# A row-maximum phase: its eight rounds rolled into loops, and the turn of the maxima moved from VectorE to TensorE

## The reference

```
xn   = layernorm(x)                                  # 4 x 2048 x 256
q, k, v = split(xn @ Wqkv.T); 16 heads of 16
dots = q k^T / 4, causal; attn = softmax(dots)
a    = (attn v) @ Wout.T + bout
h    = silu(fp4(xn) @ fp4(w_gate).T) * (fp4(xn) @ fp4(w_up).T)   # 704 wide
out  = x + a + fp4(h) @ fp4(w_down).T
```

## Time and profile before

| | |
|---|---|
| median of 3 runs | 2762.52 us (2760.96 to 2763.7) |
| the profiled execution's own time | 2762.52 us |
| its span | 2760.8 us |
| granted TensorE clock, mean over the span | 0.978 of full speed |
| busy: PE, DVE, ACT, POOL | 2562.2, 1934.7, 2038.4, 722.6 us |
| shift phase: first difference product to last join on DVE | 252.7 to 963.2 us |
| main phase: first score product | 996.4 us |

### The profile page before, as it was taken

One profiled execution on the slowest core, in us unless ns is written; L12 is line 12 of the kernel. 1 busy time (PEld: TensorE's weight loads), 2 busy tenths in 40 slices (PEclk: granted clock), 3 DMA queues, 4 the chain that ended last, 5 costly groups with the idle time before them and its releaser, 6 DMA issues.

```text
span 2760.8 us, 58289 instructions
## 1 busy us (share of the span) xinstructions
PE 2562.2 (93%) x18228; PEld 1304.5 (47%) x18228; DVE 1934.7 (70%) x5533; ACT 2038.4 (74%) x3502; POOL 722.6 (26%) x550
## 2 busy tenths in 40 slices
PE   2995999999999859999999999999999999999999
PEld 1883444444444424444454444444444445444455
DVE  7995999999999935655645656655656654566555
ACT  1554999999999847777758777775777775777775
POOL 3563334433333221122111112111121111212111
PEclk7997999999999979999999999999999999999999
DMA  2785555555445342202222112123022031220200
GB/s 70 238 272 123 75 75 75 76 72 71 71 70 72 45 84 38 51 19 39 47 78 48 32 31 46 29 58 80 22 42 43 21 76 50 40 47 23 41 24 32
DMA packets 118622, 175.70 MB, mean 64 GB/s; under 512 B 25648, under 2 KB 95024, under 8 KB 117808
## 3 DMA queue, kind: packets, MB, share of 16 engines
q1 hardware_dynamic: 97392, 147.33, 28.6%
q10 hardware_dynamic: 16576, 15.73, 2.1%
q0 software_dynamic: 4352, 8.92, 1.3%
HBM read 129.37 MB, written 42.53 MB: 62 GB/s over the span
## 4 chain that ended last, share of the span: by engine, by line
PE 54%; ACT 4%; issue 4%; SPq 1%; DMA 1%; DVE 0%; ACTq 0%; POOL 0%; DVEq 0%; POOLq 0%
PE O L923 17%; PE S L907 15%; PE F L943 10%; PE F L983 5%; ACT probs L1052 4%; PE F L973 2%; PE S L994 2%; PE S L910 2%; SPq L528 1%; PE F L936 1%; DMA y<-in_L_attn_x_dram 1%; DMA q_st<-s_shift 0%; DVE o_turned L1258 0%; ACTq L1047 0%; ACT xt_hi L1077 0%
## 5 line engine op out<-in xcount | busy, mean ns | idle before, releaser
L1052 ACT ACTIVATE probs<-S 128x1024 f32<-128x1024 f32 (+3 forms) x1280 | 1074.5, 897 | 227.6 <-PE S L910 84.1
L907 PE MATMUL S<-q_st,k_st 128*128 128x512 bf16 (+3 forms) x2560 | 648.8, 351 | 75.0 <-DMA q_st<-s_shift 38.4
L730 ACT ACTIVATE m_excess<-m_DIFF 128x512 f32<-128x512 f32 (+7 forms) x1536 | 647.1, 472 | 88.3 <-PE m_DIFF L690 42.3
L748 DVE CUSTOM_DVE_ANT_0 m_excess<-m_S,m_excess 128x512 f32<-128x512 f32 (+7 forms) x1536 | 700.7, 530 | 11.7 <-PE m_S L690 9.2
L923 PE MATMUL O<-probs,v_sb 128*32 128x512 f32 (+3 forms) x5120 | 603.6, 543 | 2.2 <-POOL v_sb L1129 2.2
L688 PE MATMUL m_S<-m_k,m_q 128*128 128x512 bf16 (+7 forms) x1536 | 483.1, 325 | 26.7 <-DVE m_row_max L748 17.3
L688 PE MATMUL m_DIFF<-m_k,m_q_diff 128*128 128x512 bf16 (+7 forms) x1536 | 478.0, 319 | 29.5 <-DMA m_q_diff<-s_q 29.2
L907 PEld LDWEIGHTS S<-q_st,k_st 128*128 128x128 bf16 x2560 | 213.7, 98 | 418.2 <-ACT probs L1052 235.1
L632 POOL TENSOR_TENSOR m_q_diff<-m_zero,m_q 48x4096 bf16<-48x4096 bf16 x32 | 224.4, 7011 | 429.0 <-DMA m_q<-s_q 418.3
L688 PEld LDWEIGHTS m_S<-m_k,m_q 128*128 128x128 bf16 x1536 | 148.3, 97 | 275.8 <-DVE m_row_max L748 194.9
L1246 DVE TENSOR_TENSOR ht_lo<-F,ht_hi 128x512 fp32r<-128x512 f32 (+1 forms) x128 | 71.0, 557 | 232.5 <-ACT ht_hi L1067 232.5
(11 more groups left out here) (163 smaller groups left out, 4189.8 us busy)
## 6 DMA issues: line engine op xcount, KB each, us to landing
k_st<-s_k SPq DMA_DIRECT2D x96, 256.0 KB, 8.6
q_st<-s_q SPq DMA_DIRECT2D x384, 64.0 KB
s_q<-a_part SPq DMA_DIRECT2D x48, 256.0 KB, 3.0
s_k<-a_part SPq DMA_DIRECT2D x48, 256.0 KB, 2.2
m_q<-s_q SPq DMA_DIRECT2D x96, 128.0 KB, 3.8
m_k<-s_k SPq DMA_DIRECT2D x96, 128.0 KB, 6.7
m_q_diff<-s_q SPq DMA_DIRECT2D x96, 128.0 KB, 8.1
m_k<-s_k SPq DMA_DIRECT2D x96, 124.0 KB, 5.2
```

The source lines that it names most:

```text
L730: act.activation(excess[u % MAX_EXCESS][:, 0:keys // 2], DIFF[u % MAX_BUFS][:, 0:keys // 2], ACT.Relu) \
L748: dve.tensor_tensor_reduce(larger, S[u % MAX_BUFS][:, 0:keys // 2], larger, 1.0, -3e38, ALU.add, ALU.max, column).then_inc(reduced[u % MAX ...
L907: ins = pe.matmul(S[half][:, s % 2, 0:st.width], k_st[p][:, s, st.j * P:(st.j + 1) * P], q_st[st.c % 2][:, s, st.skip:QC], start=True, sto ...
L1052: act.activation(probs[half][st.n % 2][:, :, 0:st.width], S[half][:, :, 0:st.width], ACT.Exp, scale=SCALE).then_inc(exped[half], 1)
```

## The change

1. The Python loops over batches and rounds of the shift phase become loops on the engines (`Fori`), on PE, ACT, DVE and SP as a loop over B with a loop over rounds in it, on POOL as one loop over the first seven rounds with the eighth behind it. Waits on semaphores inside compare with register values.
2. PE turns the table of maxima with one matmul against the identity at the end of each round, into the last difference bank (`turn`, which is `DIFF[3]`). It waits for DVE's join before it.
3. ACT makes the first part from that bank (a copy with scale -1 to bf16), and DVE the second part (`-turn - part0`). POOL's three operations and the tile `row_turned` go.
4. POOL writes each part with one transfer of 128 x 128 elements, two instead of eight per round. The wait of DVE for POOL's negation is replaced by a wait of ACT for `stored`.
5. PE waits for the last round's second part (`part1`) before the first use of `DIFF[3]` in a round.

```diff
--- before.py
+++ after.py
@@ -582,18 +582,17 @@
                               two("m_k", [P, MAX_LOAD, T], BF16))
         excess = [sb(f"m_excess{u}", [P, MAX_KEYS // 2]) for u in range(MAX_EXCESS)]
         row_max, second_max = sb("m_row_max", [P, MAX_HEADS, NKB]), sb("m_second_max", [P, MAX_HEADS, NKB - split])
-        row_turned, minus_max = sb("m_row_turned", [P, P]), sb("m_minus_max", [P, P])
-        shift_part = [sb(f"m_part{k}", [P, P], BF16) for k in range(SHIFT_PARTS)]
+        shift_part = [sb(f"m_part{k}", [MAX_HEADS * NKB, P], BF16) for k in range(SHIFT_PARTS)]
         ident_bf, future, zero = sb("m_ident", [P, P], BF16), sb("m_future", [P, P], BF16), sb("m_zero", [P, 1], BF16)
         S = [ctx.enter_context(nc.psum_tensor(f"m_S{u}", [P, MAX_KEYS // 2], F32)) for u in range(MAX_BUFS)]
         DIFF = [ctx.enter_context(nc.psum_tensor(f"m_DIFF{u}", [P, MAX_KEYS // 2], F32)) for u in range(MAX_BUFS)]
+        turn = DIFF[MAX_BUFS - 1][0:MAX_HEADS * NKB, 0:P]
         consts, zeroed, stack_ld, stack_free = once("m_consts"), [once(f"m_zeroed{p}") for p in range(2)], sems("m_stack_ld"), sems("m_stack_free")
         q_ld, q_negated = sems("m_q_ld"), sems("m_q_negated")
         differed, exceeded = sems("m_differed", MAX_BUFS), sems("m_exceeded", MAX_BUFS)
         scored, reduced = sems("m_scored", MAX_BUFS), sems("m_reduced", MAX_EXCESS)
-        joined, turned, negated, part0, part1, shift_st = (
-            sem("m_joined"), sem("m_turned"), sem("m_negated"), sem("m_part0"), sem("m_part1"), once("m_st"))
-        shift_dmas = SHIFT_PARTS * (P // SLOT)
+        joined, turned, part0, part1, stored, shift_st = (
+            sem("m_joined"), sem("m_turned"), sem("m_part0"), sem("m_part1"), sem("m_stored"), once("m_st"))
         aside = once("m_aside")
         rounds = H // MAX_HEADS
         loads = MAX_HEADS // MAX_LOAD
@@ -632,42 +631,31 @@
                 pool.tensor_tensor(q_diff[p][rows, :, :], zero[rows, 0:1].unsqueeze(2).to_broadcast([MAX_ROWS, MAX_LOAD, T]),
                                    q_st[p][rows, :, :], ALU.subtract).then_inc(q_negated[p], 1)
 
-            def store(n, negates):
-                for p in range(2):
-                    pool.wait_ge(q_negated[p], negates + PRIMED)
-                pool.wait_ge(turned, n + 1 + PRIMED)
-                pool.tensor_tensor(minus_max[:, :], zero[:, 0:1].to_broadcast([P, P]), row_turned[:, :], ALU.subtract) \
-                    .then_inc(negated, 1)
-                pool.wait_ge(negated, n + 1 + PRIMED)
-                pool.sem_inc(aside, 1)
-                pool.tensor_copy(shift_part[0][:, :], minus_max[:, :]).then_inc(part0, 1)
-                pool.wait_ge(part0, n + 1 + PRIMED)
-                pool.tensor_tensor(shift_part[1][:, :], minus_max[:, :], shift_part[0][:, :], ALU.subtract).then_inc(part1, 1)
+            def store(n):
                 pool.wait_ge(part1, n + 1 + PRIMED)
                 for k in range(SHIFT_PARTS):
-                    rows = dram["shift"][k, bass.ds(n * MAX_HEADS, MAX_HEADS), :].rearrange("h (i t) -> (h i) t", t=P)
-                    for a in range(P // SLOT):
-                        at = slice(a * SLOT, (a + 1) * SLOT)
-                        pool.dma_start(rows[:, at].rearrange("(c r) s -> r c s", r=SLOT),
-                                       shift_part[k][at, :].rearrange("r (c s) -> r c s", s=SLOT)).then_inc(shift_st, 16)
-                pool.wait_ge(shift_st, n * (16 * shift_dmas) + 16 * shift_dmas)
+                    pool.dma_start(dram["shift"][k, bass.ds(n * MAX_HEADS, MAX_HEADS), :]
+                                   .rearrange("h (i t) -> (h i) t", t=P), shift_part[k][:, :]).then_inc(shift_st, 16)
+                pool.wait_ge(shift_st, n * (16 * SHIFT_PARTS) + 16 * SHIFT_PARTS)
+                pool.sem_inc(stored, 1)
 
             pool.wait_ge(consts, 5)
             for load in range(2):
                 negate(0, load)
-            for n in range(B * rounds - 1):
+            with pool.Fori(0, B * rounds - 1) as n:
                 for load in range(2, loads):
                     negate(n, load)
                 for load in range(2):
                     negate(n + 1, load)
-                store(n, loads_before(n + 1, 1) + 1)
+                store(n)
             for load in range(2, loads):
                 negate(B * rounds - 1, load)
-            store(B * rounds - 1, loads_before(B * rounds, 0))
+            store(B * rounds - 1)
+
         @block.sync
         def _(sp):
-            for b in range(B):
-                for r in range(rounds):
+            with sp.Fori(0, B) as b:
+                with sp.Fori(0, rounds) as r:
                     n = b * rounds + r
                     for load in range(loads):
                         p = load % 2
@@ -697,6 +685,8 @@
                     pe.wait_ge(stack_ld[load % 2], loads_before(n, load) * (16 * load_dmas) + 16 * load_dmas + PRIMED)
                     pe.wait_ge(q_negated[load % 2], loads_before(n, load) + 1 + PRIMED)
                 pe.wait_ge(exceeded[u % MAX_BUFS], uses(n, u - MAX_BUFS, MAX_BUFS) + PRIMED)
+                if u == MAX_BUFS - 1:
+                    pe.wait_ge(part1, n + PRIMED)
                 product(DIFF[u % MAX_BUFS], q_diff[h // MAX_LOAD % 2], h, i, k0, keys // 2,
                         future[:, PAIR:P] if k0 + keys == (i + 1) * P else None).then_inc(differed[u % MAX_BUFS], 1)
 
@@ -708,8 +698,8 @@
                         future[:, 0:PAIR] if k0 + keys == (i + 1) * P else None).then_inc(scored[u % MAX_BUFS], 1)
 
             pe.wait_ge(consts, 5)
-            for b in range(B):
-                for r in range(rounds):
+            with pe.Fori(0, B) as b:
+                with pe.Fori(0, rounds) as r:
                     n = b * rounds + r
                     for u in range(MAX_LEAD):
                         differences(n, u)
@@ -718,10 +708,13 @@
                             differences(n, u + MAX_LEAD)
                         scores(n, u)
 
+                    pe.wait_ge(joined, n + 1 + PRIMED)
+                    pe.transpose(turn, row_max[:, :, :].rearrange("p h i -> p (h i)"), ident[:, :]).then_inc(turned, 1)
+
         @block.scalar
         def _(act):
-            for b in range(B):
-                for r in range(rounds):
+            with act.Fori(0, B) as b:
+                with act.Fori(0, rounds) as r:
                     n = b * rounds + r
                     for u, (h, i, k0, keys, _) in enumerate(round_units):
                         act.wait_ge(differed[u % MAX_BUFS], uses(n, u, MAX_BUFS) + PRIMED)
@@ -729,14 +722,17 @@
                         act.wait_ge(reduced[u % MAX_EXCESS], uses(n, u - MAX_EXCESS, MAX_EXCESS) + PRIMED)
                         act.activation(excess[u % MAX_EXCESS][:, 0:keys // 2], DIFF[u % MAX_BUFS][:, 0:keys // 2], ACT.Relu) \
                             .then_inc(exceeded[u % MAX_BUFS], 1)
+                    act.wait_ge(turned, n + 1 + PRIMED)
+                    act.wait_ge(stored, n + PRIMED)
+                    act.activation(shift_part[0][:, :], turn, ACT.Copy, scale=-1.0).then_inc(part0, 1)
 
         @block.vector
         def _(dve):
             for p in range(2):
                 for stack in (q_diff[p], q_st[p], k_st[p]):
                     dve.memset(stack[:, :, :].bitcast(F32), 0.0).then_inc(zeroed[p], 1)
-            for b in range(B):
-                for r in range(rounds):
+            with dve.Fori(0, B) as b:
+                with dve.Fori(0, rounds) as r:
                     n = b * rounds + r
                     for u, (h, i, k0, keys, second) in enumerate(round_units):
                         larger = excess[u % MAX_EXCESS][:, 0:keys // 2]
@@ -751,10 +747,9 @@
                         dve.wait_ge(reduced[buf], uses(n, len(round_units) - 1, MAX_EXCESS) + PRIMED)
                     dve.tensor_tensor(row_max[:, :, split:NKB], row_max[:, :, split:NKB], second_max[:, :, :],
                                       ALU.max).then_inc(joined, 1)
-                    dve.wait_ge(joined, n + 1 + PRIMED)
-                    dve.wait_ge(negated, n + PRIMED)
-                    dve.transpose(row_turned[:, :], row_max[:, :, :].rearrange("p h i -> p (h i)")).then_inc(turned, 1)
-                    dve.wait_ge(turned, n + 1 + PRIMED)
+                    dve.wait_ge(part0, n + 1 + PRIMED)
+                    dve.scalar_tensor_tensor(out=shift_part[1][:, :], in0=turn, scalar=-1.0, in1=shift_part[0][:, :],
+                                             op0=ALU.mult, op1=ALU.subtract).then_inc(part1, 1)
 
 
 class Step:
```

## The result

| | before | after |
|---|---|---|
| median, us | 2762.8 (2760.96 to 2763.7) | 2816.2 (2815.15 to 2817.19) |
| ratio | | 1.0188, interval 1.0175 to 1.0201 |
| span of the profiled execution, us | 2760.8 | 2810.2 |
| joins of rounds, first to last, us | 343.6 to 962.9 | 347.1 to 1020.5 |

The change costs 53.4 us. The forecast was +31.7, and 2816.2 lies above its range. The direction and the place were right. One term of the sum was too small.

What follows compares the result with a forecast made beforehand. DVE was taken to bound the shift phase. Per passage 3.9 + 0.7 + 0.5 + 0.2 = 5.3 us, for seven 37.1, less 5.45 at the phase's end, gives +31.7 on 2762.52: 2794.2 us, range 2772 to 2814.

Steps and rivals of the forecast that it cites:

- The bound and the place: Shift phase: DVE sets the pace from the first product on, and its idle time adds to the phase one to one.
- The handover: End of each round, join to turn to both parts: without branch cost, DVE starts again 1.07 us later than before.
- The fetch by itself: Loop branches at each round's end: DVE and ACT stall as in the main phase, DVE starting 3.9 us later than before.
- two things are added to each passage: From each round to the next: code fetch meeting other traffic, 0.7 us, and restarting without a lead, 0.5 us.
- the fetch meets other traffic: Branch at each round's end: code fetch runs beside SP's loads, 0.7 us a passage, bounded by 0 and doubling the 3.1 us.
- The restart of 0.5 us: Start of each next round: lost lead and PE's possibly lower clock cost 0.5 us a passage, between 0 and 1.4.
- the 0.2 for it: PE's loop branch at each round's end: 0.2 us a passage for the chance that this branch is dear.
- The end: End of the shift phase: earlier parts, six fewer transfer issues and a shorter drain save 5.45 us, between 3.95 and 7.9.
- the signs: Trace after: 93.8 us between joins, seven DVE idle times of 3 us or more, clock dips, end some 5 us shorter.
- The rival that DVE alone stalls: Branches at rounds' ends: only DVE waits for code, ACT and PE are ready; +26.5 us, 2789 us, chance 0.15.
- The heavy rival: Rounds' ends: fetch collides with loads and the clock falls, 8.4 us a passage, +53, 2816 us; chance 0.13.

Runs made afterwards that it cites:

- with the loads held: Changed kernel, with SP holding the second load of a round until DVE has reduced unit 3 of that round: 2796.2 us, 1.0123 to the kernel before.

## Why the prediction was wrong

- The bound and the place were right: DVE sets the pace, and each passage costs it what it stands idle.
- The handover was right: part 1 was over at J + 1.45 (forecast J + 1.1 to 1.4), and without loops DVE was back at J + 1.66 to 2.46 (forecast J + 1.85).
- The fetch by itself was right: J + 4.54 to 4.70 with the loads held, where I had 4.7. The stalls of the main phase's bodies of 1007 and 1030 instructions carried over to 634 and 437 (2.8 to 2.9 and 2.5 us with the loads held).
- **The step that failed** is the first of "two things are added to each passage": the fetch meets other traffic. I had 0.7 us, between 0 and 3.1. It is 7.80 - 4.62 = 3.2 us, just past its upper end. Seven times 2.5 us too little is 17 of the 22 us that are missing. I had the row for it: the DMA engines at a share of 1.06 at the end of a round. I judged by size ("a packet of 8 KB is small"), and the packets do take only some 0.4 us longer; most of the 3.2 us is waiting. Of the two behind DVE's branch the second started some 2.3 us later than with the loads held. The 0.7 itself rested on no row, and lay near the lower end though the share spoke for the upper.
- The restart of 0.5 us was 0.7 on the average of seven. PE's branch was not dear (0.21 us); the 0.2 for it cancel against this.
- The end was -8.0 and not -5.45. That takes 2.6 us off what is missing. I let the drain shrink by 1.5 us, and it shrank by 3.9, the bound. That it goes by POOL's transfers of the whole phase was not in the text.
- What else is missing of the 22 us is 3.6 us of a later start in the profiled execution and some 4 us between it and the median. Both are within the spread of what the change doesn't touch.
- Of the signs, the time between joins was 96.2 us and not 93.8, PE's branch took 0.21 us, and the granted clock did dip: 0.53 in the 11 us from the first join, where before had 1.00.
- The rival that DVE alone stalls was wrong: ACT with 437 instructions stalled in every passage, and its loop alone gave 2811.6 us. By size alone the Trainium skill, Runtime: NRT & Kernel Launch, section Instruction fetch mechanics, would have let ACT's body be held, being below its 512 instructions; the traces do not agree for ACT's 437. They do for DVE's 634 (a stall), for DVE's 320 and ACT's 218 (none), and for PE's 1365, which is below the page's 2048 (none). The forecast read the page by size. Its rule is stated for a window of two blocks of 256 instructions, and a body of 437 can touch three, so the page does not settle ACT's case.
- The heavy rival gave 2816 us and named the right mechanism, with 3.1 us for the fetch beside the loads. I gave it 0.13. That it met the median is luck: its restart was too long (1.4, measured 0.7) and its gain at the end too small (5.45, measured 8.0). Both errors make its time longer, by some 7 us together, and so stand in for the later start and the distance of the profile from the median, which it had no term for.

## What to carry to other kernels

Before rolling code into a loop, ask of each engine whether the body is held and what the DMA engines do at the moment of the branch. Here a stall of 2.3 to 2.9 us without other transfers became one of 4.2 to 7.1 us beside the 12 transfers of a load. Halving the bodies until they were held brought more (32.7 us) than moving the loads (20.0 us). Put a branch where the engine has a lead, not where three engines meet. At a barrier, look at the drain of each engine: a transfer can be cheap where it is issued and be paid for at the end of the phase.

## What was not expected of the hardware

- POOL's drain at the end of a phase took 0.06 us and 0.082 us for each transfer that POOL issued in it (16: 1.36 to 1.37, 58: 4.80, 64: 5.29), even where most of them had landed hundreds of us before. SP's took 7 ns after 442 transfers, and 0.14 us after 384 in the kernel before.
- Bodies held: PE 1365, DVE 320, ACT 218, SP 71 instructions. Not held: DVE 634, ACT 437. Where between them the limit lies was not tried.
- Two stalls at the same place are one in the time: loops on DVE alone, 2816.8 us, on all engines 2816.2 us.
- DVE's stall was 6.6 to 7.1 us where it alone looped, longer than the 5.8 to 6.2 with all engines looping, and ACT's 4.75 to 6.1 us, longer than 4.2 to 5.4. Why is open.
